# Six two-batch x buffers for the convolution of a fused AdaLN + FFN kernel, results taken earlier, and w12's first part turned in mid-stage

## The reference, cut to what matters

```python
# layer 0: a conditional 1x1 mixing of channels, then x @ kernel + bias + LoRA terms; x1 = x + that
# layer 1, conditioning: grouped convolution over the 1024 positions
out = lax.conv_general_dilated(x, weight, window_strides=(1,), padding=[(4, 4)],
                               dimension_numbers=('NCH', 'OIH', 'NCH'), feature_group_count=4)
ctx = jnp.einsum('nd,od->no', c, c_weight)
c = out + ctx[:, :, None] + bias[None, :, None]
# layer 1, FFN
x12 = jnp.einsum('bsk,mk->bsm', c, w12) + b12
x1, x2 = jnp.split(x12, 2, axis=-1)
y = x + jnp.einsum('bsm,nm->bsn', jax.nn.silu(x1) * x2, w3) + b3
```

## Time and profile before

| | |
|---|---|
| Time, median of three runs | 885.17 us (884.15 to 886.46) |
| Profiled execution: its own time, its span | 888.03 us, 886.1 us |
| TensorE busy in the span | 845.3 us (95%) |
| VectorE, ScalarE, GpSimd busy | 297.5, 134.3, 136.4 us |
| Granted TensorE clock, mean | 0.985 |

### The profile page before, as it was taken

The page is one execution under the profiler, slowest core; times in us unless marked ns, Lnnn a source line. Parts: engine busy times, 40 slices in busy tenths (PEclk is TensorE's granted clock), DMA queues, the critical chain, the costliest instruction groups (busy, mean ns, idle before and its releaser), DMA issues.

```text
span 886.1 us, 11052 instructions
## 1 busy us (share of the span) xinstructions
PE 845.3 (95%) x4177; PEld 712.0 (80%) x4177; DVE 297.5 (34%) x365; ACT 134.3 (15%) x179; POOL 136.4 (15%) x75
## 2 busy tenths in 40 slices
PE   5982999999999999999999999999999989999998
PEld 4861888888888899888888888888888868888886
DVE  3753332333231677312121213130305932222221
ACT  3421010101010233301120112010102311100000
POOL 3530323142222000000000000000000312222221
PEclk9996899999999999999999999999999999999999
DMA  8744762555447966002020202020216544444441
GB/s 246 197 134 145 212 165 74 129 134 143 117 122 168 215 144 143 13 24 72 24 71 24 72 24 74 32 71 24 71 39 176 153 131 143 142 142 148 150 149 51
DMA packets 73156, 99.92 MB, mean 113 GB/s; under 512 B 8024, under 2 KB 55560, under 8 KB 72104
## 3 DMA queue, kind: packets, MB, share of 16 engines
q1 hardware_dynamic: 71952, 98.70, 39.8%
q10 hardware_dynamic: 1032, 0.63, 0.2%
q0 software_dynamic: 144, 0.21, 0.1%
HBM read 63.45 MB, written 36.06 MB: 112 GB/s over the span
## 4 chain that ended last, share of the span: by engine, by line
PE 88%; DMA 5%; DVE 4%; SPq 2%; issue 1%; ACT 0%; DVEq 0%; ACTq 0%
PE ps L1117 88%; DMA x<-x_scratch 2%; DVE w_t L979 1%; SPq L357 1%; DMA lora_b_scratch<-lb_c_lo 1%; DVE w_lo L1000 1%; DMA lb<-lora_b_scratch 0%; DVE z L886 0%; DMA raw<-in_L_ffn_w 0%; DMA lora_b_scratch<-lbs_lo 0%; DVE h_lo L1069 0%; DVE lb_c_lo L904 0%; DMA gate_t<-in_L_ffn_gate 0%; SPq L440 0%; PE ps L1169 0%
## 5 line engine op out<-in xcount | busy, mean ns | idle before, releaser
L1117 PE MATMUL ps<-c_hi,w_hi 128*128 128x512 f32 x512 | 199.3, 389 | 0.0
L1117 PE MATMUL ps<-c_hi,w_lo 128*128 128x512 f32 x512 | 199.2, 389 | 0.0
L1117 PE MATMUL ps<-c_lo,w_hi 128*128 128x512 f32 x512 | 199.2, 389 | 0.0
L606 POOL TENSOR_TENSOR res<-x_in,b_s 128x1024 f32<-128x1024 f32 x16 | 51.0, 3193 | 535.1 <-DMA b_s<-in_L_ffn_b 413.9
L1117 PEld LDWEIGHTS ps<-c_hi,w_lo 128*128 128x128 f32 x512 | 96.1, 188 | 20.1
L1117 PEld LDWEIGHTS ps<-c_lo,w_hi 128*128 128x128 f32 x512 | 96.1, 188 | 19.9
L1117 PEld LDWEIGHTS ps<-c_hi,w_hi 128*128 128x128 f32 x512 | 96.1, 188 | 19.8
L1041 DVE SCALAR_TENSOR_TENSOR h_s<-ps,b_s,silu_s 128x512 f32<-128x512 f32 x32 | 24.0, 751 | 248.5 <-PE ps L1117 248.5
L1117 PE MATMUL ps<-w_hi,h_hi 128*128 128x512 f32 x256 | 100.2, 392 | 2.9 <-DVE w_lo L1000 2.9
L1117 PE MATMUL ps<-w_lo,h_hi 128*128 128x512 f32 x256 | 100.3, 392 | 0.0
L1117 PE MATMUL ps<-w_hi,h_lo 128*128 128x512 f32 x256 | 100.3, 392 | 0.0
(11 more groups left out here) (125 smaller groups left out, 741.7 us busy)
## 6 DMA issues: line engine op xcount, KB each, us to landing
raw<-in_L_ffn_w SPq DMA_DIRECT2D x96, 128.0 KB, 3.2
x_scratch<-x_t SPq DMA_DIRECT2D x16, 516.0 KB, 2.7
x_scratch<-x_t SPq DMA_DIRECT2D x128, 64.5 KB, 2.5
x<-x_scratch SPq DMA_DIRECT2D x16, 516.0 KB, 6.4
x_in<-x_scratch SPq DMA_DIRECT2D x16, 516.0 KB, 5.4
x_in<-in_x SPq DMA_DIRECT2D x16, 512.0 KB, 4.2
h_scratch<-h_s SPq DMA_DIRECT2D x32, 256.0 KB, 2.3
h_in<-h_scratch SPq DMA_DIRECT2D x16, 512.0 KB, 4.7
```

Of the source, the lines that this page charges most:

```text
L606: pool.tensor_tensor(res[s][:, :].rearrange("p (b h q) -> p h q b", h=2, q=4), blocks(x1_in[s]), b3_s[:, :].rearrange("p (b h q) -> p h q ...
L1117: return pe.matmul(o, l, r, start=start, stop=stop)
```

## The change

x8 becomes six buffers of two batches (one row tile) each. The first four lie where the two old ones lay; the last two lie over `x1_t`. `load_x8(t)` loads row tile t with two DMAs of 258 KB; from t = 6 on it waits for the two batches of tile t - 6. Tiles 0 to 3 are loaded before the last two stores, tiles 4 to 15 after the wait for all stores. TensorE's code for the convolution is straight, with no loop, and waits for a buffer every two batches. The `c_f` buffers move to space that is free once the last LoRA product and the last `x_plus_bias` are done, so VectorE starts its takes right behind the addition of row tile 15. VectorE turns w12's first part after 16 batches and subtracts after 24, ScalarE rounds it after 24; the wait of VectorE for all stores stands behind the last take.

```diff
-        x8 = [at(f"x8_{s}", [P, 4 * GRP, BLK + 1], 128 + 8.0625 * s) for s in range(2)]
-        c_f = [at(f"c_f{s}", [P, HALF], 144.25 + 2 * s) for s in range(4)]
+        x8 = [at(f"x8_{s}", [P, 2 * GRP, BLK + 1], 128 + 4.03125 * s) for s in range(6)]
+        c_f = [at(f"c_f{s}", [P, HALF], k) for s, k in enumerate((160.25, 162.25, 164.25, 194.25))]
...
-            def load_x8(cb, s):
-
+            def load_x8(t):
+
+                s = t % 6
+                if t >= 6:
+                    sp.wait_ge(conv_mm, 2 * (t - 6) + 2)
                 for part in range(2):
                     k0 = (part * 4 + PAD) % PH
                     sp.dma_start(x8[s][part * P // 2:(part + 1) * P // 2, :, :].rearrange("p n e -> p (n e)"),
-                                 x8_dram[k0:k0 + 4, :, ds(cb * 4 * GRP, 4 * GRP), :].rearrange("k c n e -> (k c) (n e)")
+                                 x8_dram[k0:k0 + 4, :, t * 2 * GRP:(t + 1) * 2 * GRP, :].rearrange("k c n e -> (k c) (n e)")
                                  ).then_inc(x8_loaded[s], 16)
...
-            for cb in range(2):
-                for s in range(2):
-                    sp.wait_ge(x1_stored[s], 144 * (cb + 1))
-                load_x8(cb, cb)
+            for s in range(2):
+                sp.wait_ge(x1_stored[s], 144 * 2)
+            for t in range(4):
+                load_x8(t)
             store_x1(TILES - 2, 0, TILES + 1)
             store_x1(TILES - 1, 1, TILES + 2)
             load_c_bias(1)
             for s in range(2):
                 sp.wait_ge(x1_stored[s], 144 * TILES // 2)
-            with sp.Fori(0, 3) as i:
-                for k in range(2):
-                    sp.wait_ge(conv_mm, i * 8 + 4 * k + 4)
-                    load_x8(i * 2 + 2 + k, k)
+            for t in range(4, TILES):
+                load_x8(t)
...
-            w12_hi_part(0, 0, True)
-            with act.Fori(0, 4) as i:
...
+            with act.Fori(0, 3) as i:
+                c_hi_parts(i)
+            w12_hi_part(0, 0, True)
+            c_hi_parts(3)
...
-            turn_w12(0, True)
-            w12_lo_part(0, 0)
-
-
-            for s in range(2):
-                dve.wait_ge(x1_stored[s], 144 * TILES // 2)
-
...
-            for half in range(2):
-                dve.wait_ge(c_bias_loaded[half], 16)
-                with dve.Fori(2 * half, 2 * half + 2) as i:
-                    take_c(i)
+            dve.wait_ge(xb_made, TILES)
+            dve.wait_ge(u_mm, TILES + 4)
+            dve.wait_ge(c_bias_loaded[0], 16)
+            take_c(0)
+            take_c(1)
+            turn_w12(0, True)
+            dve.wait_ge(c_bias_loaded[1], 16)
+            take_c(2)
+            w12_lo_part(0, 0)
+            take_c(3)
+            for s in range(2):
+                dve.wait_ge(x1_stored[s], 144 * TILES // 2)
...
-            def convolve(i, first=False):
-                for k in range(8):
-                    if first and k in (2, 4):
-                        pe.wait_ge(x1_made, TILES + k // 2)
-                    if k % 4 == 0:
-                        pe.wait_ge(x8_loaded[k // 4], i * 32 + 32)
-                    pe.wait_ge(c_taken, i * 8 + k + 1)
...
+            def convolve(b):
+                t = b // 2
+                if b in (2, 4):
+                    pe.wait_ge(x1_made, TILES + t)
+                if b % 2 == 0:
+                    pe.wait_ge(x8_loaded[t % 6], 32 * (t // 6 + 1))
+                pe.wait_ge(c_taken, b + 1)
...
-            convolve(0, True)
-            with pe.Fori(1, 4) as i:
-                convolve(i)
+            for b in range(NB):
+                convolve(b)
```

More of the change, by code:

```diff
@@ L223, in layered_kernel @@
         pads_made = sem("pads_made")
-        x8_loaded = [sem(f"x8_loaded{s}") for s in range(2)]
+        x8_loaded = [sem(f"x8_loaded{s}") for s in range(6)]
         conv_mm = sem("conv_mm")
@@ L715, in w12_hi_part, with c_hi_parts @@
                                    ACT.Copy).then_inc(w_hi_made, 1)
-            w12_hi_part(0, 0, True)
-            with act.Fori(0, 4) as i:
+            def c_hi_parts(i):
                 for k in range(8):
@@ L1333, in _ @@
             u_lora(u_tile(15, 1, 1, None), 15, 1, 1, 7)
-            def convolve(i, first=False):
-                for k in range(8):
-                    if first and k in (2, 4):
-                        pe.wait_ge(x1_made, TILES + k // 2)
-                    if k % 4 == 0:
-                        pe.wait_ge(x8_loaded[k // 4], i * 32 + 32)
-                    pe.wait_ge(c_taken, i * 8 + k + 1)
[L1344 to L1348, removed]
+            def convolve(b):
[5 more added lines that the diff above has]
+                pe.wait_ge(c_taken, b + 1)
+                for g in range(GRP):
+                    src, dst = x8[t % 6][:, (b % 2) * GRP + g, :], bank(b % 8)[:, g * P:(g + 1) * P]
+                    mm(dst, src[:, 0:BLK], taps[:, g, 0, :], True, False)
+                    last = mm(dst, src[:, 1:BLK + 1], taps[:, g, 1, :], False, True)
+                last.then_inc(conv_mm, 1)
             pe.wait_ge(y_taken, 2 * TILES)
-            convolve(0, True)
-            with pe.Fori(1, 4) as i:
-                convolve(i)
+            for b in range(NB):
+                convolve(b)
             def gate_step(j, s, first=False):
```

## The result

The changed kernel takes 882.12 us (median of 16 runs, 880.08 to 884.16) where the kernel before takes 885.17 (16 runs, 883.54 to 887.05). The ratio of the two is 0.9963 with a 95% interval of 0.9956 to 0.9971: a gain of 3.3 us (2.6 to 3.9); the two medians lie 3.05 us apart. Forecast were 881.7 us and a gain of 3.5. The profiled execution has a span of 880.5 us and a time of 882.35.

What follows compares the result with a forecast made beforehand. TensorE, busy 95%, was taken to bound the kernel, waiting three times for x in the convolution. Stage 60.9 becomes 57.1 + 0.2 + 0.1 = 57.4, gain 3.5: from 885.17 to 881.7 us, range 880.6 to 884.9.

Steps and rivals of the forecast that it cites:

- main case: Whole kernel: the convolution stage shrinks from 60.9 to 57.4 us, gain 3.5 us, time 881.7 us; chance 0.66.
- Three waits for x bound the stage: Convolution: TensorE waits for x before batches 8, 16 and 24 (2.16, 0.39, 0.40 us), 2.95 of 3.8 us above the floor.
- The floor of 1.785 us a batch: Convolution: TensorE's own pace once VectorE has caught up; 32 batches are 57.1 us.
- The 0.2 for the start: Convolution's first eight batches: 14.45 us instead of 14.28, added to the 57.1 us floor.
- the 0.1 for tile 4: Wait before batch 8 still expected for tile 4's load; bounds 0 and 1.9 us.
- Six buffers, small loads: x loads: issued up to five tiles (17.9 us) early, 2.2 to 2.4 us a tile against TensorE's 3.57; short waits go.
- the mechanism named for the two short waits: Before batches 16 and 24: four-batch buffer refilled only after its last batch; two DMAs take slightly longer than TensorE's four batches.
- The first wait: Before batch 8: tile 4's load issued at 303.90 again behind the stores, but half the size; wait 0.1 us instead of 2.16.
- rival 1: Before batch 8: tile 4 lands as late as the old second DMA; gain 1.6, time 883.6 us; chance 0.13.
- Takes and w12: cost 0: VectorE in the convolution: earlier takes gain nothing alone; w12's move, 4.3 + 3.5 = 7.8 us, is hidden by TensorE's banks.
- Straight code: cost 0: TensorE's convolution: 24 more batches of code in place of a loop cost 0.
- Rival 3, small loads do not overlap: x loads: each tile pays its own 5.0 us landing; stage 12.0 us late, 897.2 us; decides from 4.0 a tile; chance 0.06.

Runs made afterwards that it cites:

- e_third: The changed kernel with tiles 5 and 6 of x loaded before tile 4; ratio 1.0017 to the kernel before, stage 61.51 us.
- c_four: The changed kernel with four buffers of two batches instead of six, none over x1_t; ratio 0.9953 to the kernel before, stage 57.09 us.
- g_split: The kernel before, two buffers of four batches, each filled by four DMAs of 258 KB instead of two of 516; ratio 0.9992, stage 59.77 us.
- h_split_sp: The kernel before with each buffer filled by four DMAs of 258 KB and SyncE's refill loop written out; ratio 0.9953, stage 58.88 us.
- e_second: The changed kernel with tile 5 of x loaded before tile 4; ratio 0.9981 to the kernel before, stage 58.21 us.
- a_old_takes: The changed kernel with VectorE and ScalarE in the order of before; ratio 0.9955 to the kernel before, stage 57.09 us.
- f_w12_last: The changed kernel with w12's first part turned, rounded and subtracted behind the last take; ratio 1.0092 to the kernel before, stage 66.11 us.
- b_straight: The kernel before with only TensorE's convolution loop written out; ratio 1.0004, stage 61.61 us.
- j_takes_again: Second profile of the kernel before with only c_f's new places and VectorE's and ScalarE's new order; one execution, no ratio, stage 62.98 us.

## Why the prediction was right

The time is 882.12 us against a forecast of 881.7, and the main case is what happened. Some steps on the way to it were off.

**Three waits for x bound the stage.** Right: they are gone and the stage is 57.09 us, 0.3 under the forecast 57.4. The floor of 1.785 us a batch held: 32 of them are 57.12. The 0.2 for the start and the 0.1 for tile 4 were not needed.

**Six buffers, small loads.** Right in the sum; the depth and the mechanism of the short waits were off. The transfer was bounded by the rates of the earlier trace rows at 2.2 to 2.4 us a tile, and the landings show it: 2.3 us apart in the changed kernel, 2.2 in e_third. The depth was more than was needed: c_four shows that depth beyond four buffers does nothing. And the mechanism named for the two short waits, refills out too late, was only one way to remove them: g_split keeps the late refills and removes them by smaller DMAs, which land sooner.

**The first wait.** The step "it is issued at 303.90 again" was wrong: 8.0 us after the start and not 9.3. I had followed which instructions stand ahead of the load, and those are the same, but not what the loop's entry on SyncE's queue costs (about 0.5 us, by h_split_sp and the trace) and how fast the stores ahead are issued. It was wrong in the harmless direction. The landing was off in the same direction: the second DMA was issued 0.5 us behind the first and took 4.3 us. With an issue at 9.3 and this landing tile 4 would have had 0.1 us to spare. So the forecast of 0.1 us of wait would have been nearly right for the forecast issue, the 1.4 us of slack are mostly luck, and rival 1 was nearer than its chance of 0.13 looked. e_second is a mild form of that rival, made by hand: it loses 0.9 us of wait and 1.1 of the stage's 3.8, and by the ratios half of the gain.

**Takes and w12: cost 0.** Right, and shown from both sides: a_old_takes has the same stage, and f_w12_last gives the price of the lost cover, 9.0 us against the 7.8 that the prediction named; the last splits, 1.5 us on VectorE, were left out there. The transposes ended 35.1 us after the stage's start (forecast 35.5), the subtractions 48.2 (48.9).

**Straight code: cost 0.** Right by a 0.0 us idle time over 512 rows of straight code, and by b_straight. Of the dearer restarts with a loop that the Trainium skill's rule would allow ("Runtime: NRT & Kernel Launch", Instruction fetch mechanics) TensorE shows nothing. On SyncE's queue the loop's entry did cost about 0.5 us, but the trace shows register instructions in that time, so it does not speak for a fetch.

**Rival 3, small loads do not overlap.** It did not come: tiles landed 2.3 us apart and not 5.0, well under the 4.0 from which it decides. Smaller loads were even the better ones, 6.7 against 7.1 us for the same megabyte. The Trainium skill's rule ("DMA: Bandwidth & Descriptors", Measured) is that a DMA should be 1 MiB or more for 75% of the peak. It rests on transfers to 128 partitions issued from GpSimd, and this trace does not bear it out for loads to 64 partitions that stand behind one another on SyncE's queue.

**What was not foreseen.** Wherever the prediction priced a wait, it took its length. Each stop costs some 0.3 us besides, and a long one the clock: e_third shows that a wait of 2.5 us costs 4.4. The 1.9 us of rival 1 would have been close to the waits behind which that began (2.16 was seen both ways), with 1.6 us more to lose; then rival 1 would have ended at the time of the kernel before, not 1.6 us under it.

## What to carry to other kernels

Where a consumer waits for a double-buffered load by a few tenths of a us, cut the buffer and its DMAs in halves before finding room for more of them: the refill starts earlier and the consumer waits for half as much (c_four), and the smaller DMAs land sooner (g_split). Keep loops off the queue that issues a refill which is late. Look for how much a load has to spare, not only for whether it waits, and measure it by moving the load one place back in its queue. An idle stretch of TensorE above about 2 us may cost 1.6 us on top of its length, by the clock behind it, so of several waits the longest is worth most.

## What the hardware showed that I had not expected

- Behind waits of 2.16 to 3.40 us the granted clock of TensorE fell to 0.50, in j_takes_again over a us after work had begun again; this cost 1.6 us on top of the wait, the same in four profiles (eight batches in 16.18 us for 14.55, or 24 in 44.77 for 43.15). Another 2.16 us, in the kernel before, left the clock at 1.00.
- A stop of TensorE for a load cost 0.3 us besides its idle time (e_second: stage 1.12 us longer, wait 0.86).
- Four DMAs of 258 KB bring a megabyte about 0.4 us sooner than two of 516 KB (6.7 against 7.1 us from the first issue), although they are issued over 2.2 instead of 0.7 us.
- The entry of a loop on SyncE's queue, ahead of a DMA that had been waited for, took about 0.5 us of register instructions (303.4 to 303.90 in the kernel before; 300.6 to 300.68 without the loop).
